# Maxima over partitions by a TensorE product, quartered weight splits and a new order ahead of slot 0, in a two-layer graph kernel

## What is computed

```
h = max(layernorm(x), 0)
A = einsum('od,bdn->bon', adj, h);  C = A + b0
pre = A[:, :, None, :] + (C - A)[:, :, :, None]      # [graph, node, feature, feature]
x = x + max(relu(pre), axis=-1)                      # layer 0
h = max(layernorm(x), 0)
q, k, v = h @ Wq + bq, h @ Wk + bk, h @ Wv + bv      # 8 heads of 64
w = softmax(q k^T / 8 + mask(adj == 0))
x = x + w v                                          # layer 1
```

## Time and profile before

| | us |
|---|---|
| median of 3 runs (lowest to highest) | 1440.07 (1439.57 to 1440.17) |
| span of the profiled execution | 1438.1 |
| PE busy | 1315.2 (91%) |
| POOL busy | 1252.7 (87%) |
| DVE busy | 1120.0 (78%) |
| ACT busy | 877.0 (61%) |

### The profile page before, as it was taken

How to read it: one execution, slowest core, us unless ns; L and a number is a source line. 1 busy time by engine, 2 the same in 40 slices (tenths; PEclk the granted TensorE clock), 3 DMA queues, 4 the chain that set the end, 5 groups by cost and what they waited for, 6 DMA issues and landing times.

```text
span 1438.1 us, 32534 instructions
## 1 busy us (share of the span) xinstructions
PE 1315.2 (91%) x11137; PEld 655.8 (46%) x11137; DVE 1120.0 (78%) x1457; ACT 877.0 (61%) x1285; POOL 1252.7 (87%) x1294
## 2 busy tenths in 40 slices
PE   1569999999999999999999999999999999999962
PEld 0124444444444444444444444444444444444531
DVE  2336788888887888788988788888878788888884
ACT  2246666666666666666666666666666666666531
POOL 2178999999999999999999999999999999999731
PEclk9889999999999999999999999999999999999985
DMA  5024565555555554646464646465555555555434
GB/s 177 15 52 89 104 136 122 131 124 129 126 127 128 119 136 117 139 111 144 113 142 112 137 115 139 116 137 119 134 121 131 124 128 127 127 128 122 93 81 102
DMA packets 441372, 171.66 MB, mean 119 GB/s; under 512 B 406784, under 2 KB 406912, under 8 KB 441344
## 3 DMA queue, kind: packets, MB, share of 16 engines
q1 hardware_dynamic: 440000, 171.03, 51.3%
q10 hardware_dynamic: 1344, 0.27, 0.1%
HBM read 37.03 MB, written 33.55 MB: 49 GB/s over the span
## 4 chain that ended last, share of the span: by engine, by line
PE 51%; DMA 22%; DVE 15%; issue 8%; SPq 2%; POOL 1%; ACT 1%; DVEq 0%; POOLq 0%; ACTq 0%
PE proj L683 23%; DMA probsT<-probs 22%; PE proj L695 12%; DVE probs L506 7%; PE o_ps L727 7%; PE proj L668 6%; PE sc L712 3%; DVE attn L538 3%; SPq L236 2%; DVE a_max L492 1%; DVE out_scale L534 1%; DVE mean_var L485 1%; DVE inv_sum L532 1%; POOL h L304 0%; ACT probs L419 0%
## 5 line engine op out<-in xcount | busy, mean ns | idle before, releaser
L683 PE MATMUL proj<-hT,w 128*128 128x512 f16 x3072 | 688.0, 380 | 1.8 <-DMA hT<-h 1.8
L683 PEld LDWEIGHTS proj<-hT,w 128*128 128x128 f16 x3072 | 291.0, 98 | 351.4 <-issue 7.5
L695 PE MATMUL proj<-w,hT 128*128 128x512 f16 x1536 | 356.3, 382 | 1.5 <-DVE w L591 1.5
L335 POOL TENSOR_TENSOR qkT<-qk,qkT 128x512 f16<-128x512 f32 x256 | 298.8, 1167 | 11.6 <-ACT qk L404 11.6
L419 ACT ACTIVATE probs<-shifted 128x1024 f16<-128x1024 f32 x128 | 135.3, 1057 | 192.7 <-DMA probsT<-probs 183.6
L492 DVE TENSOR_REDUCE a_max<-proj 128x1 f32<-128x512 f32 x128 | 88.5, 691 | 204.7 <-PE proj L668 204.6
L323 POOL TENSOR_TENSOR xbv<-x_in,bv_rows 128x512 f32<-128x512 f32 x128 | 225.9, 1765 | 17.9 <-issue 7.3
L402 ACT ACTIVATE qkT<-proj,bqk_up 128x512 f16<-128x512 f32 x256 | 173.4, 677 | 109.6 <-PE proj L683 109.6
L695 PEld LDWEIGHTS proj<-w,hT 128*128 128x128 f16 x1536 | 151.0, 99 | 185.3 <-issue 5.0
L522 DVE TENSOR_TENSOR shifted<-masked,row_max 128x1024 f32<-128x1024 f32 x128 | 211.0, 1648 | 13.1 <-ACT probs L421 8.8
L314 POOL TENSOR_TENSOR y<-attn,x 128x512 f32<-128x512 f32 x128 | 162.8, 1272 | 47.5 <-DVE attn L538 47.5
(11 more groups left out here) (55 smaller groups left out, 1112.6 us busy)
## 6 DMA issues: line engine op xcount, KB each, us to landing
x_in<-in_x SPq DMA_DIRECT2D x128, 256.0 KB, 2.9
out_x<-y SPq DMA_DIRECT2D x128, 256.0 KB, 2.2
hT<-h SPq DMA_TRANSPOSE x128, 3.2
probsT<-probs SPq DMA_TRANSPOSE x128, 4.5
w_raw<-in_L_gnn_Wq SPq DMA_DIRECT2D x1, 1024.0 KB, 8.8
w_raw<-in_L_gnn_Wv SPq DMA_DIRECT2D x1, 1024.0 KB, 11.0
w_raw<-in_L_gnn_Wk SPq DMA_DIRECT2D x1, 1024.0 KB, 13.0
bv_rows<-in_L_gnn_bv ACTq DMA_DIRECT2D x1, 256.0 KB, 6.7
```

Source lines behind the costliest of these rows:

```text
L335: pool.tensor_tensor(qk_place(k, u, 1), qk32[:, u % 2, :], qk_place(k, u, 0), ALU.subtract).then_inc(qk_rest_done, 1)
L683: last = nc.tensor.matmul(proj[:, u % 2, :], w16[:, j, s, c, col * P:(col + 1) * P], hT[:, k // GROUP % 2, t, c, :, :].rearrange("p g n -> ...
L695: last = nc.tensor.matmul(proj[:, V_BANK, :], hT[:, k // GROUP % 2, s, c, k % GROUP, :], w16[:, 2, t, c, :], start=(c == 0 and i == 0), st ...
```

## The change

- `peak_over_rows` is gone from POOL. In its place PE multiplies the column `peak`, repeated over 128 columns, by the identity (`peak_to_rows`): the product, in a PSUM bank that is not yet in use, holds all 128 maxima in every partition. DVE takes the maximum along it (first instruction of the new `scales_of`).
- `scales_of` then needs two steps to `up` (mask the exponent bits, then -1 times them plus a constant, as integers' bit patterns) in place of six. The floor on the maximum is now applied per partition beforehand (`peak_floor`, `floored`).
- The split of a weight matrix is in quarters: ACT writes four heads of [128, 512], and DVE makes the rest of each as it comes.
- The rests of h of graphs 0 to 2 are made by DVE (`first_rest`), of graphs 3 and 4 still by POOL. POOL does the normalisation scales of graphs 0 to 3 in a row.
- The adjacency products of graphs 0 to 3 go to four different banks (`first_adjacency`), and no longer wait for the maximum of the one before.
- The orders of DVE and PE ahead of and in slot 0 are new. Among them: the product for Wv's maximum stands in PE's slot 0 between its two chunks, that for Wk's maximum behind slot 0; on DVE the maximum of Wk and the moments of graph 5 come after the rest of Wv.

Before, the maximum of Wk stood ahead of Wv's rest. The core of the diff:

```diff
+UP_BITS = float((2 * 127 + 14) << 23)
+PEAK_FLOOR = 2.0 ** -32
...
+        FIRST_BANKS = (proj[:, A_BANK, :], proj[:, V_BANK, :], sc[:, 0, :], sc[:, 1, :])
+        peak_rows = o_ps[:, 0, :].rearrange("p (i n) -> p i n", n=P)
...
-            def peak_over_rows(i):
-                c = MATRICES[i]
-                pool.wait_ge(peak_done, i + 1)
-                pool.partition_all_reduce(peak_all[:, c:c + 1], peak[:, c:c + 1], P,
-                                          bass.bass_isa.ReduceOp.max).then_inc(peak_all_done, 1)
-            norm_scales(0, 0)
-            peak_over_rows(0)
-            norm_scales(0, 1)
-            rest(0, 0)
-            norm_scales(0, 2)
-            rest(0, 1)
-            norm_scales(0, 3)
-            rest(0, 2)
-            peak_over_rows(1)
-            rest(0, 3)
-            peak_over_rows(2)
-            norm_scales(0, 4)
-            rest(0, 4)
-            norm_scales(0, 5)
-            peak_over_rows(3)
+            for k in range(PREP_AHEAD):
+                norm_scales(0, k)
+            pool.wait_ge(h_rest_done, DVE_RESTS)
+            for k in range(DVE_RESTS, NORM_AHEAD):
+                rest(0, k)
+                norm_scales(0, k + 1)
...
-                nc.scalar.activation(w16[:, j, 0, :, :], w_raw[:, j, :, :], ACT.Identity, scale=up[:, j:j + 1]).then_inc(heads_done, 1)
+                for c in range(KC):
+                    nc.scalar.activation(w16[:, j, 0, c, :], w_raw[:, j, c, :], ACT.Identity, scale=up[:, j:j + 1]).then_inc(heads_done, 1)
...
+            def peak_of(j, parts):
+                nc.vector.tensor_reduce(w_peak[:, j:j + 1], parts, AX.X, ALU.max, apply_absolute_value=True).then_inc(w_peak_done, 1)
+            def floored(j, i):
+                dve.wait_ge(w_peak_done, i + 1)
+                nc.vector.scalar_tensor_tensor(peak[:, j:j + 1], peak_floor[:, j:j + 1], BIAS_SHARE, w_peak[:, j:j + 1],
+                                               ALU.mult, ALU.max).then_inc(peak_done, 1)
             def w_peak_of(j, i):
                 dve.wait_ge(w_loaded[j], 16)
...
+                dve.wait_ge(peak_rows_ready, i + 1)
+                nc.vector.tensor_reduce(peak_all[:, c], peak_rows[:, i, :], AX.X, ALU.max).then_inc(peak_all_done, 1)
                 dve.wait_ge(peak_all_done, i + 1)
-                nc.vector.tensor_scalar(peak_min[:, c], peak_all[:, c], 2.0 ** -40, None, ALU.max).then_inc(scale_step, 1)
-                dve.wait_ge(scale_step, 5 * i + 1)
-                nc.vector.tensor_scalar(pow2[:, c].bitcast(U32), peak_min[:, c].bitcast(U32), EXP_BITS, None,
+                nc.vector.tensor_scalar(pow2[:, c].bitcast(U32), peak_all[:, c].bitcast(U32), EXP_BITS, None,
                                         ALU.bitwise_and).then_inc(scale_step, 1)
-                dve.wait_ge(scale_step, 5 * i + 2)
-                nc.vector.reciprocal(pow2_inv[:, c], pow2[:, c]).then_inc(scale_step, 1)
-                dve.wait_ge(scale_step, 5 * i + 3)
-                nc.vector.tensor_scalar(pow2_inv15[:, c], pow2_inv[:, c], 1.5, None, ALU.mult).then_inc(scale_step, 1)
-                dve.wait_ge(scale_step, 5 * i + 4)
-                nc.vector.tensor_scalar(pow2_invx[:, c].bitcast(U32), pow2_inv15[:, c].bitcast(U32), EXP_BITS, None,
-                                        ALU.bitwise_and).then_inc(scale_step, 1)
-                dve.wait_ge(scale_step, 5 * i + 5)
+                dve.wait_ge(scale_step, i + 1)
+                nc.vector.tensor_scalar(up[:, c].bitcast(U32), pow2[:, c].bitcast(U32), -1.0, UP_BITS,
+                                        ALU.mult, ALU.add).then_inc(scale_done, 1)
                 nc.vector.tensor_scalar(down[:, c], pow2[:, c], 1.0 / (W_SCALE * H_SCALE), None, ALU.mult).then_inc(down_done, 1)
-                nc.vector.tensor_scalar(up[:, c], pow2_invx[:, c], W_SCALE, None, ALU.mult).then_inc(scale_done, 1)
...
+                for c in range(KC):
+                    dve.wait_ge(heads_done, 2 + KC * (i - 1) + c)
+                    last = nc.vector.scalar_tensor_tensor(w16[:, j, 1, c, :], w_raw[:, j, c, :], up[:, j:j + 1],
+                                                          w16[:, j, 0, c, :], ALU.mult, ALU.subtract)
+                last.then_inc(rests_done, 1)
...
+            def first_rest(k):
+                dve.wait_ge(h32_done, k + 1)
+                dve.wait_ge(h_head_done, k + 1)
+                nc.vector.tensor_tensor(h16[:, k, 1, :], h32[:, k % 2, :], h16[:, k, 0, :], ALU.subtract).then_inc(h_rest_done, 1)
...
-            adjacency_out(0, 0)
-            w_peak_of(0, 1)
-            adjacency_out(0, 1)
+            dve.wait_ge(w_peak_done, 2)
+            nc.vector.tensor_scalar(peak_floor[:, 0:2], bqk_peak[:, :], PEAK_FLOOR, None, ALU.max).then_inc(floor_done, 1)
+            first_rest(1)
+            first_adjacency_out(0)
+            first_rest(2)
+            first_adjacency_out(1)
+            dve.wait_ge(floor_done, 2)
+            w_peak_of(0, 2)
+            first_adjacency_out(2)
             scales_of(1)
-            adjacency_out(0, 2)
-            w_peak_of(2, 2)
+            projection_scales(0, 1)
             w_rest(0, 1)
-            projection_scales(0, 1)
-            adjacency_out(0, 3)
             moments(4)
+            w_peak_of(2, 3)
+            first_adjacency_out(3)
             scales_of(2)
-            w_peak_of(1, 3)
+            projection_scales(2, 2)
             w_rest(2, 2)
-            projection_scales(2, 2)
+            w_peak_of(1, 4)
...
+            def peak_to_rows(i):
+                c = MATRICES[i]
+                pe.wait_ge(peak_done, i + 1)
+                nc.tensor.matmul(peak_rows[:, i, :], peak[:, c:c + 1].to_broadcast([P, P]), ident[:, :],
+                                 start=True, stop=True).then_inc(peak_rows_ready, 1)
+            def first_adjacency(k):
+                pe.wait_ge(h_rest_done, k + 1)
+                for i, (s, t) in enumerate(PAIRS):
+                    last = nc.tensor.matmul(FIRST_BANKS[k], adjT[:, s, :], h16[:, k, t, :],
+                                            start=(i == 0), stop=(i == 2))
+                last.then_inc(a_ready, 1)
             pe.wait_ge(ident_step, 2)
             pe.wait_ge(adj_loaded, 16)
             nc.tensor.transpose(proj[:, A_BANK, 0:P], adj_sb[:, :], ident[:, :]).then_inc(adjT_ready, 1)
+            peak_to_rows(0)
             pe.wait_ge(rests_done, 1)
-            for k in range(PREP_AHEAD):
-                adjacency(0, k)
+            first_adjacency(0)
+            first_adjacency(1)
+            first_adjacency(2)
+            peak_to_rows(1)
+            first_adjacency(3)
             def slot(base, k):
                 u = 2 * (k % GROUP)
                 scores(base, k - ATTN_BEHIND)
                 qk_chunk(base, k, u)
+                if isinstance(base, int) and base + k == 0:
+                    peak_to_rows(2)
                 qk_chunk(base, k, u + 1)
                 probs_times_v(base, k - OUT_BEHIND)
                 adjacency(base, k + PREP_AHEAD)
                 v_rows(base, k)
-            slots(pe, slot)
+            slots(pe, slot, after_first=lambda: peak_to_rows(3))
```

More of the change, by code:

```diff
@@ L48 @@
 EXP_BITS = 0x7F800000
+UP_BITS = float((2 * 127 + 14) << 23)
+PEAK_FLOOR = 2.0 ** -32
 LOAD_AHEAD, MOMENTS_AHEAD, NORM_AHEAD, TURN_AHEAD, PREP_AHEAD, X1_AHEAD = 8, 6, 5, 5, 4, 1
 ATTN_BEHIND, OUT_BEHIND, STORE_BEHIND = 5, 6, 7
+DVE_RESTS = 3
 def graph_layers(nc, x, adj, b0, wq, bq, wk, bk, wv, bv, out):
@@ L71, in graph_layers @@
         ident = sb("ident", [P, P])
-        ones = sb("ones", [P, P])
         adj_sb = sb("adj_sb", [P, P])
@@ L92, in graph_layers @@
         score_scale = sb("score_scale", [P, 1])
+        peak_floor = sb("peak_floor", [P, 4])
         bqk_peak = sb("bqk_peak", [P, 2])
-        w_peak = sb("w_peak", [P, 2])
+        w_peak = sb("w_peak", [P, 4])
         bqk_up = sb("bqk_up", [P, 2, KC])
@@ L139, in graph_layers @@
         ident_step, pool_const = sem("ident_step"), sem("pool_const")
-        peak_done, peak_all_done, scale_step, scale_done = sem("peak_done"), sem("peak_all_done"), sem("scale_step"), sem("scale_done")
+        peak_done, peak_rows_ready, peak_all_done, scale_step, scale_done = (
+            sem("peak_done"), sem("peak_rows_ready"), sem("peak_all_done"), sem("scale_step"), sem("scale_done"))
+        floor_done = sem("floor_done")
         w_peak_done, down_done, undo_done, redo_done, bias_done, score_scale_done = (
@@ L271, in _ @@
             pool.memset(plus_minus[:, 1:2], -H_SCALE).then_inc(pool_const, 1)
+            pool.memset(peak_floor[:, 2:4], PEAK_FLOOR).then_inc(floor_done, 1)
             pool.wait_ge(ident_step, 1)
@@ L550, in w_peak_of @@
                 dve.wait_ge(w_loaded[j], 16)
[L551 to L558, removed]
+                peak_of(j, w_raw[:, j, :, :].rearrange("p c n -> p (c n)"))
@@ L588, in w_rest, with first_adjacency_out @@
             def w_rest(j, i):
```

(18 more changed lines are left out.)

6 lines of the change are left out of this document (2 added, 4 removed).

## The result

The changed kernel takes **1402.34 us** (median of 4 runs, 1401.12 to 1404.0) against 1440.09 for the kernel before (4 runs); the ratio is 0.9739 [0.9725, 0.9753]. Predicted were 1402, 1396 to 1409. The profiled execution took 1401.24 us and its span is 1399.4, so 1.8 us lie outside the span.

What follows compares the result with a forecast made beforehand. PE, busy 91% of the span, was taken to bound the kernel, its full stretch starting late through POOL's gaps. Slot 2 38.0 us earlier (-21.2, -4.8, -12) gives span 1400.1, plus 1.97: 1402 us, range 1396 to 1409.

Steps and rivals of the forecast that it cites:

- The step that put the 53.9 us of gaps down to the four maxima: Prologue, POOL: eight idle gaps of at most 7.9 us around the four maxima, 53.9 us, would go with them.
- The rival without effect: POOL's gaps have another cause and stay; only 4 x 0.38 us go, 1438.5 us; chance 0.02.
- First chunk: PE's first chunk begins at 25.5 us, behind the last transpose of h, where 46.70 stood: 21.2 us earlier.
- Wq's rest: DVE's list before the first chunk: Wq's rest ready at 22.9 us, ahead of the transposes.
- The rival of late transposes: Transposes behind the loads each take full landing time: first chunk at 31.2, +5.7 us, 1408; chance 0.13, up to 1409.
- The meetings of DVE's rests with POOL's scales: Before the first chunk: up to three, some 0.6 us each, counted as nothing; all three uncovered, +1.8 us.
- Chunk 0: First chunk on PE: 12 matmuls at the low clock, 5.3 us, ending at 30.8.
- The chain behind it: From chunk 0's end at 30.8, through Wv's split, Wk's maximum and graph 5's moments and scales, to chunk 2 at 43.05.
- From chunk 2 to slot 2: PE alone decides: 8.7 us at full clock plus 1.25 for the clock, slot 2 at 53.0.
- half the price of a fallen clock: After PE's 4.7 us gap before chunk 2, a fallen clock costs +2.6 us; half was taken, 1.25.
- The sum: Slot 2 comes 38.0 us earlier (91.04 to 53.0), span 1438.1 to 1400.1, median 1.97 above it: 1402.
- The rival of a longer rhythm: Loop slots all run at 10.64 us, not 10.25: 49.5 us more, 1452; chance 0.03.

Runs made afterwards that it cites:

- Transposes first: Changed kernel, SP issuing transposes of h of graphs 0 to 3 ahead of Wk and x of graphs 4 to 7: 1399.36 us, ratio 0.9711.
- the product ahead: Changed kernel with the product for Wv's maximum moved behind the prologue's last adjacency product: 1397.27 us, ratio 0.9698.
- the moments ahead: Changed kernel, Wv's product behind the prologue's last adjacency product, graph 5's moments ahead of Wv's scale on DVE: 1394.84 us (0.9675), again 1395.96 (0.9693).
- the third comparison: Set of runs sharing the kernel before (median 1440.75 us), with the changed kernel unaltered as anchor: 1404.84 us, ratio 0.9752.
- the product alone: Kernel before with only the four maxima moved from POOL to PE products and DVE maxima, all else kept: 1397.86 us, ratio 0.9697.
- DVE's quarters above: Wv's rest in the trace of the changed kernel with transposes of h issued earlier and graph 5's moments ahead of Wv's scale: 1396.3 us, ratio 0.9691.

## Why the prediction was right

- **What goes.** The mechanism was right. The step that put the 53.9 us of gaps down to the four maxima is shown by three runs: the gaps go when only the maxima go, come back with them, and do not double when they do. The rival without effect is out. The Trainium skill's rule in "GPSIMD Engine Reference", section "Engine selection", gives this reduction to GpSimd; here leaving it brought 10.8 us per matrix on average (43.2/4), so the measurement decides against it.
- **First chunk.** Predicted 25.5, came 25.69, released by the last transpose. Wq's rest was ready at 22.1 (predicted 22.9). Transposes first moved it as worked out. The rival of late transposes (31.2) did not come: behind the loads the four took 9.9, 5.4, 3.3 and 3.9 us to land, where one took 3.1 alone, but they overlapped, and the last had landed by 25.7. The meetings of DVE's rests with POOL's scales, for which the prediction counted nothing, were two of some 0.4 us each (`h_mul` 0.62 and `var_eps` 0.65 for 0.19), and the first chunk did not wait for them.
- **Chunk 0.** This is the mis-sized term: predicted 5.3 us at the low clock, it took 3.95 to the product behind it. PE had worked on adjacency products until 18.6 and stood for 7.1 us; the clock was low at the start of the chunk and rose within it, at about 28.5. In the second profiled execution of the same kernel it took 5.28 us, as predicted. The size of this term thus differs from one execution to the next. In the first:

```profile
27.00:28.00 1.00, 1.00 (x4) 0.37 (x3) 0.00 (x0) 0.00 (x0) 0.17 (x1) 0.50 0.00 0
28.00:29.00 1.00, 1.00 (x5) 0.35 (x4) 0.00 (x0) 0.00 (x0) 0.00 (x0) 0.76 0.64 129
29.00:30.00 1.00, 1.00 (x7) 0.69 (x6) 0.00 (x0) 0.00 (x0) 0.00 (x0) 1.00 0.73 134
```

(the stretches of the kernel after; the seventh figure from the third on, behind POOL's, is the clock).

- **The chain behind it.** Predicted from 30.8 to 43.05, 12.25 us; it ran from 29.64 to 41.76, 12.1. Its parts came as worked out: from the product to Wv's rest 4.6 us (predicted 4.55), to the end of graph 5's moments 3.2 (3.5), to chunk 2 another 4.3 (4.2). That it decides is shown by the product ahead and the moments ahead: chunk 2 came 3.5 and 5.6 us earlier, in the second with no wait left.
- **From chunk 2 to slot 2.** Predicted 9.95, with half the price of a fallen clock; it took 10.1. The clock did fall, and it cost 1.6 us (24 matmuls in 7.03 us and not 5.44), between the two values that the prediction left open, 0 and 2.6. Wk's rest, for which the prediction gives 47.5 where its own terms add up to 47.75, was ready at 48.0 beside POOL's work, still ahead of slot 2.
- **The sum.** 39.2 us and not 38.0 at slot 2, by chunk 0's 1.3. It is 38.7 in the span and 37.8 in the medians. That 1402 came within 0.4 us is in part luck: the span was 0.7 us shorter than worked out, and the median lay 2.9 us above the profiled span where 1.97 was taken. In the third comparison the same kernel had 1404.84, still within the range.
- **The loop.** The mean interval is 10.24 to 10.29 us in every kernel here, whenever slot 2 began; before and after it is 10.25. The rival of a longer rhythm is out.
- **What I missed.** I worked out the chain and did not ask what the old order would have cost with the product alone. There Wv's maximum is not behind chunk 0, and the one part beats the whole change by 0.4%. The prediction names the product behind chunk 0 as a link of the chain (DVE waits for it from about 27) and does not ask whether it has to stand there.

## What to carry to other kernels

An engine that idles on both sides of one instruction, with nothing in the profile to hold it, may be paying for the change of kind, as POOL did here around its maximum over partitions (no other kind of instruction was tried). Issue it twice in a row to find out. If so, count the changes, not the instruction's own 0.4 us, and move that work to another engine. Once such a stall is gone, write down the new chain before reordering anything, and see whether a short product that stands behind a long block could stand ahead of it: one moved instruction gave 3.7 us here, more than quarters and DVE's rests together. The fastest kernel by its median is the changed one with Wv's product ahead of chunk 0 and the moments of graph 5 ahead of Wv's scale, 0.9675 and 0.9693 of the kernel before. It stands clear of the changed kernel, but not of the product alone (0.9697), whose interval overlaps both of its own.

## What the runs showed of the hardware

- A change between POOL's ordinary instructions and its maximum over partitions costs 5.9 to 7.9 us each way; a second maximum right behind the first costs 0.4 us and no stall.
- The changed kernel's own spread is in part the clock. In its second profiled execution (1407.92 us) the same first chunk, begun at 25.88, took 5.28 us and not 4.11, and chunks 2 and 3 took 8.03 and not 7.03; slot 2 came at 54.43 and not 51.86. In the first one the clock fell even after PE had resumed at 41.76:

```profile
41.00:42.00 1.00, 0.24 (x2) 0.15 (x3) 0.00 (x0) 1.00 (x3) 0.92 (x2) 1.00 0.00 0
42.00:43.00 1.00, 1.00 (x4) 0.37 (x3) 0.00 (x0) 1.00 (x3) 0.92 (x2) 0.57 0.52 94
43.00:44.00 1.00, 1.00 (x4) 0.37 (x3) 0.59 (x1) 1.00 (x3) 1.00 (x2) 0.50 0.44 168
```

  So of 24 matmuls behind a gap of 4.5 us a part ran at 1.2 GHz, and how many differed from one execution to the next. Of the 6.7 us between the two spans these are 2.6. The other 4.2 lie in the loop (its 127 intervals add up to 1306.5 and not 1302.3), and I have not traced them.
- DVE with two inputs and POOL hold each other up. In the product alone, which keeps the whole splits, POOL's 1.15 us subtraction took 3.27 us beside DVE's rest of Wk:

```profile
39.52 2.35 DVE L583 SCALAR_TENSOR_TENSOR w<-w_raw,up,w 128x2048 f16<-128x2048 f32 x1 [0.66 <-ACT w L426]
39.62 3.27 POOL L336 TENSOR_TENSOR qkT<-qk,qkT 128x512 f16<-128x512 f32 x1
```

  The Trainium skill's "SBUF — State Buffer", section "SBUF: two separate sides", says that the two exclude each other for the instruction's length; the trace agrees, the wait being the 2.1 us that DVE's instruction still had to run. In quarters the waits are shorter for POOL and longer for DVE: beside the 5.51 us of DVE's quarters above, POOL's later two additions took 1.59 and 1.37 us, where 1.27 and 1.04 stand without DVE's two-input work beside them.
